# Self-attention and a group norm over chosen channels: four split tiles in place of two, two of them on GpSimd, and every engine's work laid out by slots

## The reference

```
f = Wf x + bf;  g = Wg x + bg        (16 rows each, per image)
h = Wh x + bh                        (128 rows)
beta = softmax_j(f^T g)              (1024 x 1024 per image)
y = x + gamma * (h beta)

cos = sum over images of yn yn^T / 8   (yn: each channel row of y divided by its norm)
partners of a channel = the 3 channels with the smallest |cos| next to the first
out = gamma' * (y - mean) / sqrt(var + 1e-5) + beta'   (sums over the channel and its partners)
```

## Time and profile before

| What | us |
|---|---|
| median of 3 runs | 214.53 |
| span of the profiled execution | 211.9 |
| TensorE busy | 186.4 |
| VectorE busy | 173.7 |
| ScalarE busy | 143.9 |
| GpSimd busy | 34.3 |
| stages 1 to 6, each | 22.2 to 22.4 |

### The profile page before, as it was taken

The page is one execution under the profiler, slowest core; times in us unless marked ns, Lnnn a source line. Parts: engine busy times, 40 slices in busy tenths (PEclk is TensorE's granted clock), DMA queues, the critical chain, the costliest instruction groups (busy, mean ns, idle before and its releaser), DMA issues.

```text
span 211.9 us, 2596 instructions
## 1 busy us (share of the span) xinstructions
PE 186.4 (88%) x727; PEld 115.2 (54%) x727; DVE 173.7 (82%) x317; ACT 143.9 (68%) x256; POOL 34.3 (16%) x39
## 2 busy tenths in 40 slices
PE   7669979999999999999999999999999999983100
PEld 3435546465765676466756675657465756462000
DVE  6588989979898889979797979887988898766660
ACT  2548976799379955995499658984799378740320
POOL 0200210034003400160007100520034001001400
PEclk9999999999999999999999999999999999997555
DMA  6240002500060007000520052002200020000198
GB/s 207 89 162 0 0 0 100 203 0 0 39 257 3 0 0 292 6 0 3 205 94 0 0 186 111 0 0 99 99 0 0 3 99 0 0 0 0 53 403 336
DMA packets 4904, 16.16 MB, mean 76 GB/s; under 512 B 544, under 2 KB 672, under 8 KB 4896
## 3 DMA queue, kind: packets, MB, share of 16 engines
q1 hardware_dynamic: 4320, 14.68, 18.4%
q10 hardware_dynamic: 576, 1.38, 1.7%
HBM read 4.52 MB, written 4.19 MB: 41 GB/s over the span
## 4 chain that ended last, share of the span: by engine, by line
PE 71%; DVE 13%; ACT 6%; issue 5%; POOL 1%; DVEq 0%; ACTq 0%; POOLq 0%
PE o_ps L636 40%; PE s_ps L617 11%; PE w_ps L611 6%; PE w_ps L606 6%; DVE nmax L404 3%; PE w_ps L651 3%; ACT probs L318 3%; PE w_ps L645 2%; PE o_ps L603 2%; DVE y_all L596 1%; DVE probs_low L418 1%; DVE g_parts L427 1%; DVE y_cur L447 1%; ACT probs_high L324 1%; DVE values L435 1%
## 5 line engine op out<-in xcount | busy, mean ns | idle before, releaser
L318 ACT ACTIVATE probs<-s_ps,nmax 128x1024 f32<-128x1024 f32 x64 | 70.9, 1108 | 40.5 <-DVE nmax L404 40.5
L636 PE MATMUL o_ps<-probs,vnorm 128*128 128x512 f32 x192 | 90.2, 594 | 0.5 <-DVE y_cur L447 0.5
L404 DVE TENSOR_REDUCE nmax<-s_ps 128x1 f32<-128x1024 f32 x64 | 77.9, 1218 | 10.2 <-PE s_ps L617 9.8
L617 PE MATMUL s_ps<-g_parts,f_parts 128*128 128x512 f32 x128 | 51.6, 485 | 4.6 <-ACT probs L318 2.3
L636 PEld LDWEIGHTS o_ps<-probs,vnorm 128*128 128x128 f32 x192 | 35.3, 189 | 28.8 <-issue 23.2
L266 POOL TENSOR_TENSOR f_parts<-fg,fg_neg 64x512 fp32r<-64x512 f32 x14 | 24.0, 1713 | 122.1 <-ACT fg_neg L311 122.1
L617 PEld LDWEIGHTS s_ps<-g_parts,f_parts 128*128 128x128 f32 x128 | 21.2, 190 | 20.7 <-issue 14.0
L418 DVE TENSOR_TENSOR probs_low<-probs,probs_high 128x1024 fp32r<-128x1024 f32 x16 | 19.5, 1221 | 1.3 <-ACT probs_high L324 1.2
L427 DVE TENSOR_TENSOR g_parts<-fg,fg_neg 64x512 fp32r<-64x512 f32 x16 | 13.9, 871 | 6.6 <-ACT fg_neg L311 6.5
L335 ACT ACTIVATE vnorm<-values,rinv 128x128 f32<-128x128 f32 x48 | 18.8, 391 | 0.0
L611 PEld LDWEIGHTS w_ps<-wd,x_cur 128*128 128x128 f32 x112 | 14.7, 192 | 6.7 <-issue 6.7
(11 more groups left out here) (90 smaller groups left out, 165.7 us busy)
## 6 DMA issues: line engine op xcount, KB each, us to landing
x_all<-x_dram SPq DMA_DIRECT2D x7, 512.0 KB, 4.0
x_cur<-x_all SPq DMA_DIRECT2D x7, 512.0 KB, 3.2
y_all<-y_cur SPq DMA_DIRECT2D x7, 512.0 KB, 2.9
out_dram<-y_all SPq DMA_DIRECT2D x5, 512.0 KB, 5.8
out_dram<-y_all ACTq DMA_DIRECT2D x2, 512.0 KB, 4.1
x_all<-x_dram SPq DMA_DIRECT2D x2, 256.0 KB, 3.7
out_dram<-y_all SPq DMA_DIRECT2D x2, 256.0 KB, 2.2
wd<-wide_dram ACTq DMA_DIRECT2D x1, 256.0 KB, 4.3
```

Of the source, the lines that this page charges most:

```text
L318: nc.scalar.activation(probs[t][:, :], s_ps[t % 2][:, :], ACT.Exp, bias=nmax[:, t:t + 1], accum_out=rsum[:, t:t + 1]).then_inc(exp_done, 1)
L404: nc.vector.reduce_max(nmax[:, t:t + 1], s_ps[t % 2][:, :], AX_X, negate=True).then_inc(max_ready, 1)
L617: last = nc.tensor.matmul(s_ps[t % 2][:, h], f_parts[par][:, t * P:(t + 1) * P], g_parts[par][:, h], start=True, stop=True)
L636: last = nc.tensor.matmul(o_ps[:, halves[h]], weights[:, :], rows[:, halves[h]], start=(t == 0 and n == 0), stop=(t == T - 1 and n == len( ...
```

## The change

There are now four split tiles, 2, 3, 6 and 7. Tiles 3 and 6 have their probabilities split by ScalarE and VectorE, tiles 2 and 7 by GpSimd. The reciprocal moves from the values to the probabilities of split tiles: ScalarE's `probs_high` is scaled as it is rounded, VectorE's `probs_low` is one scalar_tensor_tensor, and GpSimd scales, copies and subtracts in three instructions. The values of the split tiles are split once for each half image, on GpSimd, unscaled. Whole tiles are as before.

f and g come straight from PSUM: ScalarE makes the negated high part (`negate_high`), and one VectorE instruction per half makes the parts of both, 128 rows. The g rows then lie in the wrong partitions, and a DMA moves them to `g_low` for all images but the first.

The loop, `x_cur`, `y_cur` and `y_all` are gone; the residual is written over x. All engines walk the same slots, one per tile from -4 on, and constants say in which slot each job is issued. `AHEAD` is 4.

```diff
-AHEAD = 3
-SCALED = 2
-SPLIT = (3, 7)
+AHEAD = 4
+SCALE_LAG = 1
+LOW_LAG = 2
+VECTOR_SPLIT = (3, 6)
+POOL_SPLIT = (2, 7)
+SPLIT = (2, 3, 6, 7)
+
+PE_FG, ACT_NEG, DVE_PARTS = (0, 1), (0, 0), (1, 1)
+PE_V, DVE_V, POOL_V = (4, 5), (5, 5), (5, 6)
+
+PE_T, ACT_T, DVE_T = (2, 3), (1, 3), (3, 4)
+ACT_SQUARE, POOL_NORM = 4, 4
+PE_GRAM, DVE_GRAM, PE_TURN, DVE_ADD = 6, 6, 7, 8
...
+            for b in range(1, B):
+
+                for h in range(H):
+                    sp.wait_ge(parts_ready, H * b + h + 1)
+                    if b >= 2:
+                        sp.wait_ge(scores, T * (b - 1))
+                    sp.dma_start(g_low[b % 2][0:KP, halves[h]].bitcast(F32),
+                                 fg_parts[b % 2][KP:P, halves[h]].bitcast(F32)).then_inc(g_in[h], 16)
+                if b + 2 < B:
+                    load(b + 2)
...
+            def split_values(b, h):
+                tiles = SPLIT_VALUES[h]
+                source = values[b % 2][:, tiles, :]
+                pool.wait_ge(v_ready, H * b + h + 1)
...
+                nc.gpsimd.tensor_copy(v_high[b % 2][:, tiles, :], source).then_inc(vh_ready, 1)
+                pool.wait_ge(vh_ready, H * b + h + 1)
+                nc.gpsimd.tensor_tensor(v_low[b % 2][:, tiles, :], source,
+                                        v_high[b % 2][:, tiles, :].bitcast(F32),
+                                        ALU.subtract).then_inc(vl_ready, 1)
+
+            def split_probs(b, t):
+                n, count = SPLIT.index(t), pool_split_count(b, t)
+                pool.wait_ge(rinv_ready, T * b + t + 1)
+                nc.gpsimd.tensor_scalar(probs[t][:, :], probs[t][:, :], rinv[:, t:t + 1], 1.0,
+                                        ALU.mult, ALU.mult).then_inc(pool_scaled, 1)
+                pool.wait_ge(pool_scaled, count)
+                nc.gpsimd.tensor_copy(probs_high[n][:, :], probs[t][:, :]).then_inc(pool_high, 1)
+                pool.wait_ge(pool_high, count)
+                nc.gpsimd.tensor_tensor(probs_low[n][:, :], probs[t][:, :], probs_high[n][:, :].bitcast(F32),
+                                        ALU.subtract).then_inc(pool_low, 1)
...
+            for slot in range(-AHEAD, T * B):
+                b, t = divmod(slot, T)
+                its = tile_at(slot + AHEAD - 1)
+                if its is not None and its[1] in POOL_SPLIT:
+                    split_probs(*its)
+                for h in range(H):
+                    if slot == -1 and b < 0:
+                        split_values(0, h)
+                    if b >= 0 and b < L and t == POOL_V[h]:
+                        split_values(b + 1, h)
...
+            def low_part(b, t):
                 n = SPLIT.index(t)
...
+                dve.wait_ge(high_ready, vector_split_count(b, t))
+                nc.vector.scalar_tensor_tensor(probs_low[n][:, :], probs[t][:, :], rinv[:, t:t + 1],
+                                               probs_high[n][:, :].bitcast(F32), ALU.mult,
+                                               ALU.subtract).then_inc(low_ready, 1)
+
+            def parts(b, h):
+                dve.wait_ge(neg_ready, H * b + h + 1)
+                if b >= 2:
+                    dve.wait_ge(scores, T * (b - 1))
+                nc.vector.scalar_tensor_tensor(fg_parts[b % 2][:, halves[h]], w_ps[:, halves[h]], wd[:, BFG:BFG + 1],
+                                               fg_neg[:, halves[h]].bitcast(F32), ALU.add,
+                                               ALU.add).then_inc(parts_ready, 1)
...
+            for slot in range(-AHEAD, T * B):
+                b, t = divmod(slot, T)
+                its = tile_at(slot + AHEAD)
+                if its is not None:
+                    score(*its)
+                for h in range(H):
+                    if 0 <= b < L and t == PE_FG[h] == 0:
+
+                        project_fg(b + 1, h)
...
+                if slot >= 0:
+                    attend(b, t)
+                for h in range(H):
+                    if 0 <= b < L and t == PE_FG[h] > 0:
+                        project_fg(b + 1, h)
+                    i = before(b, t, PE_T[h])
+                    if i is not None:
+                        transposes(i, h, w_ps[:, halves[h]])
+                    if 0 <= b < L and t == PE_V[h]:
+                        project_values(b + 1, h, w_ps)
+                i = before(b, t, PE_GRAM)
```

More of the change, by code:

```diff
@@ L191, in build, with split_values_of, tile_at, before @@
         GROUPS = [slice(0, 1), slice(1, 3), slice(3, B)]
+        WHOLE = [t for t in range(T) if t not in SPLIT]
+        def split_values_of(h):
+            its = [t for t in SPLIT if t // TH == h]
+            step = its[1] - its[0] if len(its) > 1 and len({b - a for a, b in zip(its, its[1:])}) == 1 else 1
+            return slice(its[0], its[-1] + 1, step)
+        SPLIT_VALUES = [split_values_of(h) for h in range(H)]
         def shifts_for(b):
             return next(n for n, g in enumerate(GROUPS) if b < g.stop) + 1
[L196 to L206, removed]
+        def tile_at(slot):
+            return divmod(slot, T) if 0 <= slot < T * B else None
+        def before(b, t, slot):
+            i = b - 1 - slot // T
+            return i if slot % T == t and 0 <= i < L else None
+        def vector_split_count(b, t):
+            return len(VECTOR_SPLIT) * b + VECTOR_SPLIT.index(t) + 1
+        def pool_split_count(b, t):
+            return len(POOL_SPLIT) * b + POOL_SPLIT.index(t) + 1
         def whole_count(b, t):
             return len(WHOLE) * b + WHOLE.index(t) + 1
[L211 to L219, removed]
         block = ctx.enter_context(nc.Block())
@@ L258, in _ @@
             pool.wait_ge(halves_set, 1)
[L260 to L265, removed]
-                    nc.gpsimd.tensor_tensor(f_parts[b % 2][0:KP, halves[h]], fg32[0:KP, halves[h]],
-                                            fg_neg[0:KP, halves[h]].bitcast(F32), ALU.add).then_inc(f_ready, 1)
-            pool.wait_ge(neg_ready, H)
@@ L280, in _, with norm @@
+            def norm(b):
                 if b < L:
@@ L420, in split_parts @@
-                dve.wait_ge(vh_ready, split_count(b, t))
-                nc.vector.scalar_tensor_tensor(v_low[n][:, :], values[par][:, t, :], rinv[:, t:t + 1],
-                                               v_high[n][:, :].bitcast(F32), ALU.mult,
-                                               ALU.subtract).then_inc(vl_ready, 1)
-            def parts(to, rows, columns, done):
-                nc.vector.tensor_tensor(to[0:KP, columns], fg32[rows, columns], fg_neg[rows, columns].bitcast(F32),
-                                        ALU.add).then_inc(done, 1)
@@ L451, in low_part, with residual @@
-            def low_part(tiles, source):
+            def residual(b, h):
+                if h == 0:
+                    dve.wait_ge(first_half, b + 1)
+                else:
+                    dve.wait_ge(probs_used, T * (b + 1))
+                nc.vector.scalar_tensor_tensor(x_all[:, b, halves[h]], o_ps[:, halves[h]], wd[:, GAMMA:GAMMA + 1],
+                                               x_all[:, b, halves[h]], ALU.mult, ALU.add,
+                                               accum_out=sums[:, h, b:b + 1]).then_inc(y_ready, 1)
@@ L528, in _ @@
-            scale_gram(L - 1, w_ps)
-            for h in range(H):
-                dve.wait_ge(yT_high, L + 1 + h)
-                low_part(slice(h * TH, (h + 1) * TH), s_ps[h][:, halves[0]])
-            add_gram(L - 1, w_ps[:, BANK:BANK + P])
+            nc.vector.tensor_tensor(bias_neg[:, :], wd[:, BFG:BFG + 1], wd[:, NMASK:NMASK + 1],
+                                    ALU.mult).then_inc(bias_set, 1)
+            first_g(0)
+            parts(0, 0)
+            first_g(1)
+            parts(0, 1)
```

490 lines of the change are left out of this document (220 added, 270 removed).

## The result

The changed kernel takes 213.46 us (median of 13 runs, 213.03 to 214.53) against 214.55 us before (13 runs, 214.19 to 215.03). The ratio is 0.995 with an interval of 0.9938 to 0.9963: faster by 1.1 us, clear of the noise but only half a per cent. The changed kernel's executions spread with their mean granted clock: 213.03 to 213.46 us at 0.942 to 0.944, 213.62 to 214.53 at 0.929 to 0.936. I had predicted 212.0, a gain of 2.5. The range (208.8 to 219) was wide enough to hold the time. That the total is off by only 1.5 us is partly luck: against the forecast the head is 2.55 us worse and the middle 1.2 better.

The account below looks back on a forecast made before the run. TensorE was taken as the bound, full in a 22.2 us middle stage. Middle -2.7, head -0.1 and last stage +0.2 gave -2.6, from 214.5 to 212.0 us; range 208.8 to 219, forecast's own 210.3 to 213.6.

Parts of the forecast that it names:

- the head: Stretch up to image 0's residual: stage 0 ending at 35.6 against 36.25, -0.65, with 0.5 given back, so -0.1 us.
- The direction: Whole kernel: faster with chance 0.64, same 0.06, slower 0.30.
- stage 0's TensorE work: In the head: a stage's 21.55 us less transposes, gram and turn, 19.6, starting at about 16.0 and ending at 35.6.
- the 0.5 that the text gave back: In the head: GpSimd does tile 2 before splitting the values, ready after tile 2 is due; 0.5 us (0 to 2).
- The stalls given back: Middle stages: 0.2 us each (0 to 1.0) for tile 2, g's move and the residual, leaving -2.7 over six.
- rival A: Everything hidden, one-input GpSimd work at 1.2 us and no late g: middle -3.9, total 209.1 us; chance 0.15.
- the lock: VectorE's probs_low meeting GpSimd on shared ports: each waits 0 to 2.3 us, taken as 0.8; GpSimd delayed up to 1.22.
- Move of g: DMA of 128 KB for the next image: some 1.9 us, leaving 0.9 to spare before its tile 0 is scored.
- Rival C: g late after VectorE waits 2.3 us before tile 3's probs_low; scores stand 1.0 us per stage: 216.7 us; chance 0.10.
- Tile 2's lateness: Middle stages: a GpSimd tile of 5.5 us fits tile 2's 6.5 us window; with a lock, 6.7, 0.2 over.
- rival B: GpSimd the new bound through a tile's three instructions, decided by tile plus lock over 7.15 us: 219 us; chance 0.20.
- Last stage: Last stage and tail: -1.1 us, with 1.3 given back for tile 7 waiting on GpSimd, so +0.2.

Follow-up runs that it names:

- e5: Changed kernel with tiles 2 and 7 whole, so two split tiles of eight and none on GpSimd, which still splits values: 216.47 us, 1.0078.
- e2: Changed kernel with 8, 2 and 4 spare bf16 matmuls behind scores 1, 2 and 3 in the head, no real work moved: 211.70 us, 0.9855.
- e9: Changed kernel with image 1's f and g projected behind score 1, six spare matmuls behind the fourth score, last image's tile 7 whole: 209.87 us, 0.9775.
- e11: e9 with GpSimd splitting the values of image 0 before it takes up tile 2: 209.6 us, 0.9767.
- e1: Changed kernel with f and g of image 1 projected in the head behind score 1, not in slots 0 and 1: 211.77 us, 0.9869.
- e13: e6 with ScalarE's squares in slot 2 and GpSimd's norm in slot 3, ahead of tile 7's split: 221.5 us, 1.0314.
- e6: Changed kernel with GpSimd's rounding copy done twice for tiles 2 and 7: 224.39 us, 1.0445.
- e4: Changed kernel with the gram of image 6 scaled behind the last residual instead of before it: 212.99 us, 0.9921.
- e3: Changed kernel with tile 7 of the last image whole, its probabilities not split on GpSimd: 211.99 us, 0.988.
- e12: Changed kernel with GpSimd splitting the values of image 0 before tile 2, nothing else edited: 212.94 us, 0.9918.

## Why the prediction was right and wrong

**The direction was right, and so was its ground.** The two tiles cost TensorE 0.66 us less, and e5 takes just that away again. The floor of 21.55 is met to 0.01 us in five of the six.

**The step that failed is the head.** The prediction gave it -0.1; measured are +2.45. Its first half held: slot 0, which begins with score 4, was to start at about 16.0, and score 4 started at 16.36. What failed is the next term, stage 0's TensorE work of 19.6 us with 0.5 given back, 20.1 in all. From score 4 to the score that opens the next stage (38.85) it took 22.5. The term was added up from the prices of a middle stage, at a granted clock of 1.00, and put the clock at nothing. The text counted what was added in front of tile 0, and not what left: image 1's projection had filled TensorE's first gap. Moving it away left idle time, and behind it the clock was 0.75 and 0.64. e2 prices the clock alone at 1.72 of the 2.45 us. The granted clock of 0.63 in the idle tail stood in the earlier trace rows, and I never asked in which other stretch TensorE would be as thin.

The other 0.7 is the sum of several small terms. Against the kernel before, the first score won 1.40 (I had 1.7). With the clock mended, tile 2 of image 0 waits for the values that GpSimd splits behind it, the 0.5 that the text gave back: e9 to e11 price it at 0.58. That it is also what e1 and e2 have left is read from their waits of 0.97 and 0.82; no run removed it there. What the later exponentials cost is open.

**The stalls given back, 0.2 per stage, did not come.** On the middle rival A was right: -3.89, where the prediction had -2.7. The size of a term was wrong here, not its sign. Three prices were too high. A one-input instruction of 128x1024 takes GpSimd 1.04 to 1.12 us alone, under my lower end of 1.2 and far from the chosen 1.5. A tile takes 4.7 us, not 5.5. And the lock costs VectorE's `probs_low` 0.08 on average (1.366 against 1.283), not 0.8: 13 of the 16 take 1.28 or 1.29.

The lock is there, in both orders. VectorE and GpSimd of the kernel after, first a middle stage, then stage 0:

```profile
94.67 1.28 DVE L417 SCALAR_TENSOR_TENSOR probs_low<-probs,rinv,probs_high 128x1024 fp32r<-128x1024 f32 x1
```

```profile
94.68 2.18 POOL L266 TENSOR_SCALAR probs<-probs,rinv 128x1024 f32<-128x1024 f32 x1 [7.69 <-DVE rinv L412]
```

```profile
31.08 1.12 POOL L266 TENSOR_SCALAR probs<-probs,rinv 128x1024 f32<-128x1024 f32 x1 [6.99 <-DVE rinv L412]
31.32 1.95 DVE L417 SCALAR_TENSOR_TENSOR probs_low<-probs,rinv,probs_high 128x1024 fp32r<-128x1024 f32 x1 [0.34 <-ACT probs_high L338]
```

In the middle VectorE is first by 0.01 us, and GpSimd's 1.12 become 2.18. In stage 0 GpSimd is first, and VectorE's 1.28 become 1.95. In the last stage GpSimd's copy takes 1.90 and not 1.04. It costs the path nothing in the middle, as GpSimd has the slack. But tile 2's subtraction ends at 108.54 and VectorE's `probs_low` begins at 108.50, so the dear meeting is missed by a hair; e13 shows it. In each meeting the second to start waits for about the rest of the first, which is what the Trainium skill says of the shared ports (SBUF — State Buffer, "Who interferes with whom"). And its GPSIMD Engine Reference, section 4.1, says that one-input work is near line rate and two-input work about twice as slow as on VectorE: the trace agrees with both, 1.04 for the copy and 2.37 against 1.28 for the subtraction. The prediction had the rule and weighed it too little.

**Move of g.** It landed in 2.2 us, not 1.9, and no score of a middle stage waits for it. Rival C fell for this kernel; the meeting that it starts from, VectorE held up by GpSimd's subtraction before `probs_low` of tile 3, happened in e13, for 1.0 us and not 2.3.

**GpSimd's slack.** Tile 2's lateness and rival B's threshold were worked out per tile. The tightest path was another, the norm behind tile 7 to VectorE's gram with 0.3 us to spare (e6, e13). By this slack a tile dearer by a few tenths of a microsecond would have shown it; that is reckoned, no run was so fine.

**Last stage.** The text gave back 1.3 for tile 7. Measured are 0.80 of wait and 0.6 through the norm (e4), 1.4 together, and e3 wins 1.6 with both gone, though its whole tile costs TensorE 0.33 more; the rest is not parted. The size was nearly right, the second cause unseen. With the stretch to the last byte the change is +0.54, where I had +0.2.

**Outside the span** 1.8 us stand where 2.6 were taken over. Every kernel without the loop has about 1.8 (1.75 to 1.84 in thirteen profiles); that the loop is the cause is only argued.

## What to carry to other kernels

When an order is rewritten, list for each gap of the bounding engine what filled it before; a job that leaves an idle stretch can cost the granted clock for the work behind it, here 1.7 us. Count a helper engine's slack to everything in its queue, the small instructions behind the large one too, and follow them to who waits. When a sum agrees with a measurement, look in the trace whether the wait that it names is there (e13). An idle GpSimd can be worth using, a two-input subtraction included: here it took two tiles in eight and the bounding engine stayed at its floor, but in short last stages, where nothing covers it, the same tile is better kept whole.

## What the runs showed of the hardware

- The granted clock fell after idle times of 2.08, 0.40 and 0.94 us between short scores, and in e1 it was 0.88 and 0.81 after 0.37, 0.40 and 1.42 us. For e1 I had expected 1.00. Fourteen spare matmuls, whose results nobody reads, kept it at 1.00 and gave 1.7 us.
- A wait can hide behind the slow clock: before tile 2 of image 0 TensorE waited 2.55 us at 1.00 (e9) and not at all in the changed kernel, where removing its cause gave 0.08 us (e12).
- VectorE and GpSimd hold each other up in both orders: 1.12 us became 2.18 on GpSimd, 1.28 became 1.95 and, in e13, 2.29 on VectorE.
- GpSimd: 128x1024 scaled by a column of scalars 1.12 us, copied 1.04, subtracted 2.37; 128x256 copied 0.40, subtracted 0.74.
- The best kernel, e11, keeps the change in the middle, mends the head and leaves the last tile whole: 209.6 us, 0.9767 of before.
